# Mixing weights from 16 products over 32 rows, and a tail for the first expert

## The chip, the cores and the metric

The kernel runs on one core of a Trainium2 chip. The time is the device time of one execution in microseconds (us). A run also leaves a profile of one execution, which has a time of its own. Engines are named as in the profile: PE (TensorE, the matmuls), PEld (its weight loads), DVE (VectorE), ACT (ScalarE), POOL (GpSimd), SP (SyncE, which here only issues DMAs).

## What is computed

Two layers of the same form. A mixing step makes a new activation from x, a mixture-of-experts step turns it into an update, and the update is added to x. The change touches only the first layer:

```
att   = softmax(mlp(cond))                        # 32 samples x 8 kernels
agg_w = einsum('bk,koi->boi', att, weight)        # a 64 x 64 mixing matrix for each sample
c0    = einsum('boi,bih->boh', agg_w, x) + att @ bias_k
logits = c0 @ gate_w                              # 2048 tokens, 8 experts
topv, topi = top_k(logits, 2);  w = softmax(topv)
x = x + sum over the two experts e of a token:  w_e * (c0 @ expert_w[e])
```

x is 32 samples x 64 channels x 1024, so 2048 tokens of 1024 features. The second layer mixes with a grouped convolution, has one shared 1024 x 1024 product and LoRA products for each expert.

## The kernel before

Tokens lie in 16 tiles of 128 rows (two samples each).

**Start.** SP loads constants, tile 0, more constants, tile 1, the mixing kernels `kern` (four DMAs of 8 partitions each, line 453), then tiles 2 to 15. PE computes the small network for `att` (lines 1321 to 1325). ACT and DVE make `att_rep`, the attention repeated in four groups of 8 rows, and a product with the identity turns it (L1408) into `att_t`. PE transposes tile 0 and tile 1, four 128 x 128 blocks at a time (`turn_x`, L1339), and ACT copies each batch out of the one bank that they share (`take_turned`, L746), so PE's next batch waits for ACT. Then come 64 mixing products (L1425): for each of 16 output channels o of a group and each of four row groups g, 8 rows of kernels (stationary, 128 columns) times 8 rows of `att_t` (moving, 32 columns). They fill banks 0 to 3. ACT (L767) and DVE (L935) spread these into `bd`, block-diagonal matrices. `gate_products(0)` (L1353) needs all four batches of the first two tiles, and everything of the loop needs `bd`.

**Loop.** For each pair of tiles: transposes, gate products, mixing (`mix`, L1376), logits, top 2, ranks, and the lists of tokens by expert. ACT stores c0 to DRAM. Beside it expert 0's weights are split into a rounded part `w_hi` and the rest `w_lo`.

**Experts.** The tokens of an expert are worked off in slots of 128. POOL gathers the rows of a slot from DRAM (`gather`, L640), one slot ahead, into the one buffer `xg`. PE transposes them in the middle of the slot before (`transposes`, L1472), ACT and DVE split them into `l_hi` and `l_lo`, and PE runs 2 x 24 products of 128 x 512 (`product`, L1481). Meanwhile the weights of the next expert are rounded by ACT (`round_w`, L798) and their rest is made by DVE (`rest_w`, L1098), while SP loads those of the expert after. For experts 2 to 7, the last up to 32 tokens of an expert, its tail, can be left out of the slots: they are gathered together (L668, two gathers, issued by POOL between the slots of expert 0 and those of expert 1, once expert 1's weights are all split, `s_lo`), turned in `turn_tails` (L1508, L1514) behind expert 0's last slot, copied by ACT (L847) and DVE (L1119, L1122), and multiplied in fp32 with the raw weights, in four column groups of 32 (`tail`, L1529), half before and half after the first slot of the expert before. ACT evicts a tail (`take_tail`, L810) and stores it. The number of slots of an expert is computed on the chip: one for each 128 begun, of its count less 32 where it has a tail, at least 3 for experts 0 and 7 and 2 for the others. With the inputs here there are 33 slots, 5 of them expert 0's.

**Order.** Each engine's queue is written out by hand and runs in order; semaphores tie them together. After the experts come the sum of the two experts' rows for each token, and the second layer (conv L1561, down L1570, main L1481, up L1577).

Of the kernel before, what the change touches and what calls it, by code (L numbers as in the profile page):

```python
# [24 lines left out]
TAIL, PLAIN = 32, 2  # L25
GROUPED = E - PLAIN
# [22 lines left out]
QO = CH // QUAD  # L49
# [5 lines left out]
def columns(widths):  # L55

    at, out = 0, {}
    for name, w in widths:
# [7 lines left out]
                    ("thr", NT - 1), ("cw", CH), ("fside", CH), ("tok", NT), ("pick", E)])  # L66
# [32 lines left out]
def build(nc, x, x_t, kern, x_ph, consts_a, consts_b, expert_w, conv_w, down_w, lora_b, out):  # L99
    ctx = ExitStack()  # L100
    with ctx:
# [12 lines left out]
        y_d = dram("y_scratch", [(SLOTS + 1) * P + (E - 2) * TAIL, H])  # L114
# [42 lines left out]
        def row(i, n=1):  # L157
            return work[:, i * H:(i + n) * H]
# [5 lines left out]
        kern_sb = row(4, 2).rearrange("p (o i) -> p o i", o=QO)  # L164
# [29 lines left out]
        att_rep = early[0:B, 10 * P:11 * P]  # L194

# [15 lines left out]
        tail_out = sb("spare", [P, SPARE])[:, 0:H // QUAD]  # L211
        scratch = sb("scratch", [P, E * HG])
        attx = scratch[0:B, :].rearrange("p (n k) -> p n k", k=K8)
        att_t = sb("att_t", [P, B])
# [30 lines left out]
        tail_f = sb("tail_f", [P, GROUPED])  # L245
# [100 lines left out]
        s_txt = [sem(f"s_txt_{j}") for j in range(3)]  # L346
        s_tprod = sem("s_tprod")
        s_tev = sem("s_tev")
# [52 lines left out]

        def places(e):

            return max(e - 1, 0) * TAIL if isinstance(e, int) else e * TAIL - TAIL
# [34 lines left out]
        def _(sp):  # L439
# [53 lines left out]
            sp.wait_ge(s_tplace, 2)  # L493
# [11 lines left out]
            def late_loads():  # L505
# [3 lines left out]
                behind = sp.value_load(cum[0:1, PLAIN:PLAIN + 1], min_val=sum(LEAST[:PLAIN]), max_val=SLOTS)  # L509
                sp.dma_start(y_d[bass.ds(sp.snap(behind * P), TAIL), :], ca[0:TAIL, 0:H]).then_inc(s_rest, 16)  # L510
# [9 lines left out]
            def fill(part):  # L520
# [3 lines left out]
                with sp.Fori(*at) as g:  # L524
                    sp.dma_start(y_d[bass.ds(sp.snap(g * P + (E - 2) * TAIL), P), :], ca[:, 0:H]).then_inc(s_rest, 16)
# [5 lines left out]
            def expert(e, first, last, between=None):  # L531
# [9 lines left out]
                if not last:  # L541
# [5 lines left out]
                    if first:  # L547

                        sp.wait_ge(s_tturn, 3)
                    load_raw(nxt2, range(4, 6))  # L550

            def first_rows():

                sp.wait_ge(s_tprod, 2 * GROUPED)
# [73 lines left out]
        def _(pool):  # L628
            pool.memset(att_rep, 0.0).then_inc(s_init, 1)
# [67 lines left out]
            pool.wait_ge(s_tst, 16 * GROUPED + DMA_CREDIT)  # L697
# [25 lines left out]
        def _(act):  # L723

            act.wait_ge(s_init, 5)
# [36 lines left out]
            for n in range(4):  # L762
                take_turned(0, n)
# [983 lines left out]
```

## Time and profile before

| | us |
|---|---|
| median of 3 runs | 816.88 |
| lowest, highest | 813.99, 818.6 |
| profiled execution, its time | 816.01 |
| profiled execution, its span | 814.3 |

The span runs from the first to the last instruction. Its stages: start to about 26 us, loop to 98, experts to 518, then the second layer. A name such as L1425 is a line of the kernel. In the rows, `out<-in` are the program's names, `x128` is a number of instructions (an fp32 product is recorded as two matmuls and two weight loads), and a bracket gives the idle time of the engine ahead of the row and what ended it. A busy engine that is not on the chain of work that ended last costs nothing.

### The profile page before, as it was taken

The page shows a single profiled execution, that of the slowest core. Times are in us where ns is not written, and L with a number is a line of the kernel's source. Part 1 is how long each engine was busy: PE and PEld are TensorE (multiplying, and loading weights), DVE is VectorE, ACT ScalarE, POOL GpSimd, SP SyncE. Part 2 cuts the span into 40 slices and gives each one's busy share as a digit, 9 for nine tenths or more (in the row PEclk, how much of TensorE's full clock was granted, in tenths as well). Part 3 has the DMA queues.
Part 4 walks back from the last instruction along what each step waited for, and adds up shares of the span by engine and source line. Part 5 has one row for each costly group of instructions (what it writes and reads, how often), then busy time and mean ns, then how long its engine had stood idle before and what let it go on. Part 6 is the DMA issues. An engine that isn't in the chain of part 4 may idle for free.

```text
span 814.3 us, 13091 instructions
## 1 busy us (share of the span) xinstructions
PE 792.2 (97%) x4450; PEld 646.0 (79%) x4450; DVE 394.7 (48%) x921; ACT 208.1 (26%) x326; POOL 86.2 (11%) x130
## 2 busy tenths in 40 slices
PE   7999899999999999999999999999999999999997
PEld 5555588778777787787877878888898889889886
DVE  1488733241331512315123153386676757678883
ACT  3444233341332523325233151300100001001200
POOL 1000112001101111011110112221112111100000
PEclk9999999999999999999999999999999999999999
DMA  9998398468474583745537255765544664432065
GB/s 269 392 342 308 114 320 318 144 196 313 127 273 162 186 324 118 269 174 173 202 111 260 93 182 168 240 178 129 126 103 113 152 148 103 106 98 56 1 219 195
DMA packets 62924, 152.77 MB, mean 188 GB/s; under 512 B 7192, under 2 KB 24616, under 8 KB 61960
## 3 DMA queue, kind: packets, MB, share of 16 engines
q1 hardware_dynamic: 42928, 99.31, 38.1%
q0 software_dynamic: 9616, 34.88, 13.8%
q10 hardware_dynamic: 10344, 18.10, 6.0%
q8 instruction: 22, 0.36, 0.2%
q14 instruction: 14, 0.11, 0.0%
HBM read 99.43 MB, written 44.44 MB: 177 GB/s over the span
## 4 chain that ended last, share of the span: by engine, by line
PE 91%; DMA 4%; DVE 1%; ACT 1%; issue 1%; SPq 1%; POOL 0%; ACTq 0%; POOLq 0%; DVEq 0%
PE bank L1481 63%; PE bank L1561 6%; PE bank L1570 4%; PE bank L1472 4%; PE bank L1376 4%; PE bank L1529 3%; PE bank L1577 3%; DMA work<-c_scratch,idx 2%; PE bank L1353 1%; PE bank L1400 1%; DMA work<-y_scratch,pos_c 1%; PE bank L1425 1%; PE bank L1339 1%; DMA x1p<-res 1%; PE bank L1365 1%
## 5 line engine op out<-in xcount | busy, mean ns | idle before, releaser
L1481 PE MATMUL bank<-weights,l_hi 128*128 128x512 f32 x1568 | 483.3, 389 | 0.0
L1481 PEld LDWEIGHTS bank<-weights,l_hi 128*128 128x128 f32 x1568 | 294.4, 188 | 59.5
L1481 PE MATMUL bank<-weights,l_lo 128*128 128x512 f32 x784 | 311.1, 397 | 1.1 <-DVE l_lo L1065 1.1
L1481 PEld LDWEIGHTS bank<-weights,l_lo 128*128 128x128 f32 x784 | 147.3, 188 | 34.7 <-issue 6.2
L1065 DVE TENSOR_TENSOR l_lo<-bank,l_hi 128x512 fp32r<-128x512 f32 x33 | 22.9, 693 | 185.7 <-ACT l_hi L786 185.7
L1098 DVE TENSOR_TENSOR weights<-work,weights 128x1024 fp32r<-128x1024 f32 x48 | 55.9, 1220 | 23.1 <-ACT weights L798 23.1
L1561 PE MATMUL bank<-conv_sb,x1p 128*128 128x128 f32 x512 | 59.8, 275 | 2.5 <-DMA x1p<-res 1.3
L1561 PEld LDWEIGHTS bank<-conv_sb,x1p 128*128 128x128 f32 x512 | 58.7, 192 | 3.0 <-DMA x1p<-res 1.6
L640 POOL DMA_INDIRECT work<-c_scratch,idx x33 | 34.4, 1043 | 233.4 <-PE bank L1472 139.9
L1223 DVE TENSOR_TENSOR res<-bank,res 128x512 f32 (+1 forms) x30 | 31.9, 1064 | 54.5 <-PE bank L1481 43.5
L1070 DVE TENSOR_TENSOR l_lo<-bank,l_hi 128x512 fp32r<-128x512 f32 x33 | 22.8, 692 | 64.7 <-ACT l_hi L791 64.7
L872 ACT ACTIVATE l_hi<-work 128x512 fp32r<-128x512 f32 x32 | 18.4, 623 | 134.2 <-PE bank L1481 128.0
L798 ACT ACTIVATE weights<-work 128x1024 fp32r<-128x1024 f32 x48 | 47.3, 1047 | 16.1 <-issue 15.7
L786 ACT ACTIVATE l_hi<-bank 128x512 fp32r<-128x512 f32 x34 | 20.4, 599 | 101.9 <-PE bank L1481 92.3
L830 ACT ACTIVATE work<-bank 128x512 f32<-128x512 f32 x33 | 19.6, 595 | 93.9 <-PE bank L1481 83.0
L791 ACT ACTIVATE l_hi<-bank 128x512 fp32r<-128x512 f32 x34 | 20.3, 598 | 70.0 <-PE bank L1481 70.0
L1570 PE MATMUL bank<-down_sb,work 128*128 128x160 f32 x256 | 37.5, 299 | 0.6 <-DVE hb L1189 0.6
L1175 DVE TENSOR_TENSOR work<-bank,ctxb 128x512 f32<-128x512 f32 x32 | 33.5, 1130 | 8.6 <-PE bank L1561 7.8
L1472 PEld LDWEIGHTS bank<-ca,work 128*128 128x128 f32 x272 | 31.7, 140 | 7.5 <-issue 2.3
L1570 PEld LDWEIGHTS bank<-down_sb,work 128*128 128x128 f32 x256 | 36.1, 190 | 1.9 <-issue 0.8
L1472 PE MATMUL bank<-ca,work 128*128 128x128 f32 x272 | 35.4, 272 | 2.1 <-DMA work<-c_scratch,idx 2.1
L690 POOL DMA_INDIRECT work<-y_scratch,pos_c x32 | 33.0, 1031 | 26.2 <-POOL pos_c L685 9.7
(204 smaller groups left out, 603.2 us busy)
## 6 DMA issues: line engine op xcount, KB each, us to landing
work<-in_expert_w SPq DMA_DIRECT2D x52, 512.0 KB, 5.6
y_scratch<-work ACTq DMA_DIRECT2D x66, 256.0 KB, 3.4
x1p<-in_expert_w SPq DMA_DIRECT2D x20, 512.0 KB, 8.0
y_scratch<-ca SPq DMA_DIRECT2D x18, 512.0 KB, 10.1
res<-in_x SPq DMA_DIRECT2D x16, 512.0 KB, 15.1
c_scratch<-work SPq DMA_DIRECT2D x16, 512.0 KB, 3.7
res<-in_x_ph SPq DMA_DIRECT2D x14, 512.0 KB, 5.6
x1p<-res SPq DMA_DIRECT2D x112, 64.0 KB, 4.8
```

The costliest lines, as they stand in the source:

```text
L640: pool.indirect_dma_start(xg, None, c0_d, bass.IndirectOffsetOnAxis(ap=idx[:, 0:1], axis=0)).then_inc(s_xg, 16)
L690: pool.indirect_dma_start(yg[j][:, k, :], None, y_d, bass.IndirectOffsetOnAxis(ap=pos_c[j][:, k:k + 1], axis=0)).then_inc(s_yg[j][k], 16)
L798: act.activation(w_hi[1 - odd][:, at, :], raw[buffer(at)], ACT.Copy).then_inc(s_hi, 1)
L1098: dve.tensor_tensor(w_lo[1 - odd][:, at, :], raw[buffer(at)], w_hi[1 - odd][:, at, :].bitcast(F32), ALU.subtract).then_inc(s_lo, 1)
L1175: dve.tensor_tensor(out4[:, b], ps, add.unsqueeze(2).to_broadcast([P, CQ, HC, CP]), ALU.add).then_inc(s_c1, 1)
L1223: dve.tensor_tensor(to[:, w, :], bank[h][:, :].rearrange("p (w q) -> p w q", q=PH), rows[:, w, :], ALU.add).then_inc((s_me0, s_me1)[h], 1)
L1376: mm = pe.matmul(bank[2 * j + h][:, :], bd[:, t, :], x_sb[t][:, h * HALF:(h + 1) * HALF], start=True, stop=True)
L1472: mm = pe.transpose(bank[bk][:, k * P:(k + 1) * P], xg[:, at * P:(at + 1) * P], ident)
L1481: mm = pe.matmul(to[:, :], a[:, k, :], b[:, k, cols * HALF:(cols + 1) * HALF], start=(k == 0 and n == 0), stop=(k == HC - 1 and n == 2 and ...
L1529: mm = pe.matmul(bank[4][g * TAIL:(g + 1) * TAIL, 0:H // QUAD], tail_xt[:, e - PLAIN, k, :], raw[buffer(k)][:, g * (H // QUAD):(g + 1) * ( ...
L1561: mm = pe.matmul(bank[to + b][:, at:at + P], x1p[j][:, b, u, m * P + k:(m + 1) * P + k], conv_sb[:, k, u, :], start=(k == 0), stop=(k == W ...
L1570: mm = pe.matmul(bank[2][:, 0:G1W], c1_of(t)[:, k, :], down_sb[:, k, :], start=(k == 0), stop=(k == HC - 1))
```

## The change

**Mixing weights.** The 8 kernels of four output channels are laid into the 32 rows of a row group, so 16 products take the place of 64: 32 rows of kernels (stationary, 128 columns) times 32 rows of `att_own` (moving, 128 columns), which is the attention repeated over all rows and multiplied by a mask (`own`) that keeps it in the columns of its own channel. The kernels are loaded by one DMA over 128 partitions, ahead of tile 1. The products stand ahead of tile 1's transposes in PE's queue, and ACT's block copies stand between and behind the copies of tile 1's last batches. POOL's memset of `att_rep` is dropped.

**First expert's tail.** Expert 0 gets a tail too. Its rows are gathered as the seventh tail, in the second gather. It is multiplied behind `turn_tails` with `w_hi[0]` and `w_lo[0]`, read as fp32, both into bank 5 (`first_tail`, 64 products), since the raw weights are gone by then. All four copies of turned tails are waited for. ACT evicts bank 5 and stores it, and expert 2's tail on PE waits for that eviction. Places and counts follow: a tail's rows stand behind each expert but expert 1.

```diff
             load_x(0)
             sp.dma_start(ca[:, mlp:CA_W], consts_a[:, mlp:CA_W]).then_inc(s_const, 16)
+            sp.dma_start(kern_sb, kern.rearrange("p (o i) -> p o i", o=QUAD)).then_inc(s_kern, 16)
             load_x(1)
-            for g in range(QUAD):
-                sp.dma_start(kern_sb[g * QP:g * QP + K8, :, :], kern[g, :, :].rearrange("k (o i) -> k o i", o=QO)).then_inc(s_kern, 16)
...
@@ scalar
-            for n in range(4):
+            for n in range(3):
                 take_turned(0, n)
             act.wait_ge(s_pe0, 7)
-            for g in range(QUAD // 2, QUAD):
-                for b in range(2):
-                    act.activation(*block(g, b), ACT.Copy).then_inc(s_bda, 1)
+            for b in range(2):
+                act.activation(*block(QUAD - 2, b), ACT.Copy).then_inc(s_bda, 1)
+            take_turned(0, 3)
+            for b in range(2):
+                act.activation(*block(QUAD - 1, b), ACT.Copy).then_inc(s_bda, 1)
...
-            act.wait_ge(s_tturn, 1)
-            act.activation(tail_xt[:, 0:QUAD, 0:HC // 2, :], bank[4][:, :].rearrange("p (k i m) -> p i k m", k=HC // 2, i=QUAD),
-                           ACT.Copy).then_inc(s_txt[0], 1)
-            with act.Fori(0, GROUPED // 2) as pair:
+            for n in (0, 2):
+                act.wait_ge(s_tturn, n + 1)
+                act.activation(*turned_tails(n), ACT.Copy).then_inc(s_txt[n], 1)
+            act.wait_ge(s_tprod0, 1)
+            act.activation(first_tail_out, bank[5][:, 0:H // QUAD], ACT.Copy).then_inc(s_tev, 1)
+            act.wait_ge(s_tev, 1)
+            rows = bass.ds(act.snap(act.value_load(cum[0:1, 1:2], min_val=LEAST[0], max_val=SLOTS) * P), TAIL)
+            act.dma_start(y_d[rows, :].rearrange("r (g n) -> g r n", g=QUAD), first_tail_out).then_inc(s_tst0, 16)
+            with act.Fori(0, E // 2 - 1) as pair:
...
@@ vector
-            dve.tensor_copy(att_t[:, :], bank[6][:, 0:B]).then_inc(s_att, 1)
+            dve.tensor_tensor(att_own.rearrange("p (o n) -> p o n", o=QUAD), bank[6][:, 0:B].unsqueeze(1).to_broadcast([P, QUAD, B]),
+                              c("own").unsqueeze(2).to_broadcast([P, QUAD, B]), ALU.mult).then_inc(s_att, 1)
...
-            ch.add(dve.tensor_tensor(cmp[:, 0:PLAIN, :], bank[4][:, 0:PLAIN].unsqueeze(2).to_broadcast([P, PLAIN, NT - 1]),
-                                     c("thr").unsqueeze(1).to_broadcast([P, PLAIN, NT - 1]), ALU.is_gt))
...
+            for some in (slice(0, 1), slice(2, E)):
+                n = some.stop - some.start
+                ins = dve.scalar_tensor_tensor(cmp[:, some, :], bank[4][:, some].unsqueeze(2).to_broadcast([P, n, NT - 1]),
+                                               float(-TAIL), c("thr").unsqueeze(1).to_broadcast([P, n, NT - 1]),
+                                               ALU.add, ALU.is_gt)
...
@@ tensor
+            pe.wait_ge(s_kern, 16)
+            pe.wait_ge(s_att, 2)
+            pe.wait_ge(s_ctx0, 1)
+            for o in range(QUAD):
+                for g in range(QUAD):
+                    rows = slice(g * QP, (g + 1) * QP)
+                    mm = pe.matmul(bank[g][:, o * P:(o + 1) * P], kern_sb[rows, o, :], att_own[rows, :], start=True, stop=True)
+            mm.then_inc(s_pe0, 1)
             turn_x(0, 2)
             turn_x(0, 3)
-            pe.wait_ge(s_kern, 16 * QUAD)
-            pe.wait_ge(s_att, 2)
-            pe.wait_ge(s_ctx0, 1)
-
-            for o in range(QO):
-                for g in range(QUAD):
-                    rows = slice(g * QP, g * QP + K8)
-                    mm = pe.matmul(bank[g][:, o * B:(o + 1) * B],
-                                   kern_sb[rows, o, :],
-                                   att_t[rows, :], start=True, stop=True)
-            mm.then_inc(s_pe0, 1)
             gate_products(0)
...
             def tail(e, half):
-                if e == PLAIN:
-                    for taken in s_txt[0:1] if half == 0 else s_txt[1:]:
-                        pe.wait_ge(taken, 1)
-                elif half == 0:
-
-                    pe.wait_ge(s_tev, e - PLAIN)
+                if half == 0:
+
+                    pe.wait_ge(s_tev, e - 1)
...
+            def first_tail():
+
+                for taken in s_txt:
+                    pe.wait_ge(taken, 1)
+                for k in range(HC):
+                    for n, part in enumerate((w_hi[0], w_lo[0])):
+                        for g in range(QUAD):
+                            mm = pe.matmul(bank[5][g * TAIL:(g + 1) * TAIL, 0:H // QUAD], tail_xt[:, TAILED.index(0), k, :],
+                                           part[:, k, g * (H // QUAD):(g + 1) * (H // QUAD)].bitcast(F32),
+                                           start=(k == 0 and n == 0), stop=(k == HC - 1 and n == 1))
+                mm.then_inc(s_tprod0, 1)
...
             one_expert(pe, experts_slot, 0, 0)
             turn_tails()
+            first_tail()
```

## Rows read from the trace of the kernel before

**Rows 1.** Page, parts 1 and 4: busy time of engines; chain that ended last

```profile
PE 792.2 (97%) x4450; PEld 646.0 (79%) x4450; DVE 394.7 (48%) x921; ACT 208.1 (26%) x326; POOL 86.2 (11%) x130
...
PE 91%; DMA 4%; DVE 1%; ACT 1%; issue 1%; SPq 1%; POOL 0%; ACTq 0%; POOLq 0%; DVEq 0%
```

**Rows 2.** Busy time by stretch: us, engines (instructions), clock, DMA share, GB/s

```profile
9.00:12.00 3.00, 3.00 (x11) 1.84 (x9) 0.48 (x3) 0.60 (x1) 0.00 (x0) 1.00 0.97 128
...
26.00:98.00 72.00, 65.39 (x368) 38.11 (x368) 54.77 (x275) 30.51 (x46) 2.18 (x2) 1.00 0.77 291
```

**Rows 3.** Timeline, start: start us, us, engine, line, operation, [idle before <- releaser]

```profile
12.40 1.12 PE L1339 MATMUL bank<-ca,res 128*128 128x128 f32 x4
...
13.55 0.60 ACT L746 ACTIVATE work<-bank 128x512 f32<-128x512 f32 x1 [3.89 <-PE bank L1339]
...
14.20 1.11 PE L1339 MATMUL bank<-ca,res 128*128 128x128 f32 x4 [0.69 <-ACT work L746]
...
15.25 7.05 PE L1425 MATMUL bank<-att_t,work 8*128 8x32 f32 x128
...
22.23 1.90 PE L1353 MATMUL bank<-work,ca 128*8 128x256 f32 x16
...
22.77 1.19 ACT L767 ACTIVATE bd<-bank 64x256 f32<-64x256 f32 x3
...
25.84 3.27 PE L1376 MATMUL bank<-res,bd 128*128 128x512 f32 x4
...
29.75 1.10 PE L1376 MATMUL bank<-res,bd 128*128 128x512 f32 x2
```

**Rows 4.** Source lines 1425 and 1481: weight loads, duration ns min/median/max

```profile
L1425 PEld LDWEIGHTS bank<-att_t,work x128: 283/328/328, 15.2 to 21.8; 8*128 8x128 f32 x128
...
L1481 PEld LDWEIGHTS bank<-weights,l_hi x1568: 187/188/192, 98.3 to 808.6; 128*128 128x128 f32 x196
```

**Rows 5.** Chain that ended last: start us, us, what; slots and a tail half

```profile
128.35 10.90 PE bank L1481 x48
...
140.13 10.90 PE bank L1481 x48
...
173.83 1.86 PE bank L1529 x32
```

**Rows 6.** Timeline: the tails' copy on ACT and the first tail products

```profile
159.23 0.60 ACT L847 ACTIVATE work<-bank 128x512 f32<-128x512 f32 x1 [0.68 <-PE bank L1514]
...
159.88 1.93 PE L1529 MATMUL bank<-work 128*32 128x256 f32 x32 [1.00 <-ACT work L847]
```

**Rows 7.** Timeline of POOL: the row gathers of expert 0

```profile
117.36 1.05 POOL L640 DMA_INDIRECT work<-c_scratch,idx  x1 [2.01 <-PE bank L1472]
...
125.65 0.34 POOL L654 COPY idx<-idx_all 128x1 int32 x1 [7.24 <-DMA work<-c_scratch,idx]
...
137.73 0.94 POOL L668 DMA_INDIRECT x1p<-c_scratch,tail_idx  x1 [7.54 <-issue]
...
139.88 0.19 POOL L654 COPY idx<-idx_all 128x1 int32 x1
...
141.02 0.97 POOL L640 DMA_INDIRECT work<-c_scratch,idx  x1 [0.95 <-PE bank L1472]
...
147.02 0.18 POOL L654 COPY idx<-idx_all 128x1 int32 x1 [5.03 <-DMA work<-c_scratch,idx]
```

**Rows 8.** Timeline: last rest of expert 1's weights; transposes in slot 3

```profile
127.00 2.35 DVE L1098 TENSOR_TENSOR weights<-work,weights 128x1024 fp32r<-128x1024 f32 x2
...
139.09 1.03 PE L1472 MATMUL bank<-ca,work 128*128 128x128 f32 x8
```

**Rows 9.** Busy time by stretch, columns as in rows 2, over those gathers

```profile
128.00:136.00 8.00, 8.00 (x39) 6.66 (x37) 2.74 (x4) 1.89 (x4) 1.05 (x1) 1.00 0.98 394
```

**Rows 10.** Timeline of ACT: a tail's eviction, its store, the next eviction

```profile
179.37 0.36 ACT L810 ACTIVATE spare<-bank 128x256 f32<-128x256 f32 x1
...
182.15 0.60 ACT L830 ACTIVATE work<-bank 128x512 f32<-128x512 f32 x1 [2.42 <-PE bank L1481]
```

More of the change, by code:

```diff
@@ L24 @@
 FILLS = 4
[L25 to L26 removed]
+TAIL = 32
+TAILED = [2, 3, 4, 5, 6, 7, 0]
+GROUPED = len(TAILED)
 HC = H // P
@@ L345, in build @@
         s_tturn = sem("s_tturn")
-        s_txt = [sem(f"s_txt_{j}") for j in range(3)]
+        s_txt = [sem(f"s_txt_{j}") for j in range(4)]
         s_tprod = sem("s_tprod")
+        s_tprod0 = sem("s_tprod0")
+        s_tst0 = sem("s_tst0")
         s_tev = sem("s_tev")
@@ L508, in late_loads @@
                 sp.wait_ge(s_const, 16)
[L509 to L510 removed]
+                behind = sp.value_load(cum[0:1, 2:3], min_val=sum(LEAST[:2]), max_val=SLOTS)
+                sp.dma_start(y_d[bass.ds(sp.snap(behind * P + TAIL), TAIL), :], ca[0:TAIL, 0:H]).then_inc(s_rest, 16)
                 sp.dma_start(cb[:, :], consts_b).then_inc(s_late, 16)
@@ L810, in take_tail @@
                 act.activation(tail_out, bank[4][:, 0:H // QUAD], ACT.Copy).then_inc(s_tev, 1)
-                wait_apart(act, s_tev, e)
-                behind = act.value_load(cum[0:1, bass.ds(e + 2, 1)], min_val=PLAIN, max_val=SLOTS)
-                rows = bass.ds(act.snap(behind * P + e * TAIL), TAIL)
+                wait_apart(act, s_tev, e + 1)
+                behind = act.value_load(cum[0:1, bass.ds(e + 2, 1)], min_val=sum(LEAST[:3]), max_val=SLOTS)
+                rows = bass.ds(act.snap(behind * P + e * TAIL + TAIL), TAIL)
                 act.dma_start(y_d[rows, :].rearrange("r (g n) -> g r n", g=QUAD), tail_out).then_inc(s_tst, 16)
@@ L1117, in _ @@
                 rest_b(g + 1)
-            dve.wait_ge(s_tturn, 2)
-            dve.tensor_copy(tail_xt[:, 0:QUAD, HC // 2:HC, :],
-                            bank[5][:, :].rearrange("p (k i m) -> p i k m", k=HC // 2, i=QUAD)).then_inc(s_txt[1], 1)
-            dve.wait_ge(s_tturn, 3)
-            dve.tensor_copy(tail_xt[:, QUAD:GROUPED, :, :],
-                            bank[6][:, :].rearrange("p (k i m) -> p i k m", k=HC, i=GROUPED - QUAD)).then_inc(s_txt[2], 1)
-            with dve.Fori(0, GROUPED // 2) as pair:
+            for n in (1, 3):
+                dve.wait_ge(s_tturn, n + 1)
+                dve.tensor_copy(*turned_tails(n)).then_inc(s_txt[n], 1)
+            with dve.Fori(0, E // 2 - 1) as pair:
                 for odd in (1, 0):
@@ L1528, in tail @@
                     for g in range(QUAD):
-                        mm = pe.matmul(bank[4][g * TAIL:(g + 1) * TAIL, 0:H // QUAD], tail_xt[:, e - PLAIN, k, :],
+                        mm = pe.matmul(bank[4][g * TAIL:(g + 1) * TAIL, 0:H // QUAD], tail_xt[:, TAILED.index(e), k, :],
                                        raw[buffer(k)][:, g * (H // QUAD):(g + 1) * (H // QUAD)], start=(k == 0), stop=(k == HC - 1))
                 mm.then_inc(s_tprod, 1)
+            def first_tail():
+                for taken in s_txt:
+                    pe.wait_ge(taken, 1)
+                for k in range(HC):
+                    for n, part in enumerate((w_hi[0], w_lo[0])):
[4 more added lines that the diff above has]
+                mm.then_inc(s_tprod0, 1)
             def experts_slot(g, e, odd, first):
-                tailed = first and PLAIN <= e + 1 < E
+                tailed = first and 2 <= e + 1 < E
                 if tailed:
```

91 lines of the change are left out of this document (47 added, 44 removed).

## Prediction

> **What bounds the kernel now.** I read the page first: the tensor engine (PE) is busy for 97% of the span and is 91% of the chain that ended last [rows 1]. So time goes only where PE has less to do or stops waiting, and each part of the change has to be looked up in its own stretch. The busy times by stretch show that the loop over the tiles (26 to 98 us) holds PE for 65.4 of 72 us, with DMA at 0.77 of its engines and the vector engine (DVE) at 54.8 [rows 2]. PE sets its pace too, so what the start gains is carried through. Then comes the timeline of the start. PE turns tile 1 in two batches (12.40 and 14.20), each followed by a copy on the scalar engine (ACT), runs the 64 mixing products in 7.05 us, and ends with the first gate products at 24.13 [rows 3]. A reader should see that nothing lies between these pieces. Last, the chain in the experts' stage: one slot is 48 products and 8 transposes, and begins every 140.13 - 128.35 = 11.78 us [rows 5].
>
> **Part 1, the mixing products.** Removed: 64 products, which the trace records as 128 (two for each fp32 product), 7.05 us [rows 3]. Added: 16 products, 32 records, each with 128 moving columns where there were 32. A record of 512 columns takes 3.27/4 = 0.82 us in this stretch [rows 3], so one of 128 takes 0.20 and 32 in a row 6.5 us. The four row groups can run abreast. The nearest row is that of the gate products: they run in four column groups, their 16 records of 256 columns would be 16 x 0.41 = 6.5 us in a row and took 1.90, which is 3.4 abreast [rows 3]. By this the new products take 6.5/3.4 = 1.9. The bounds are 1.6 (four abreast) and 6.5 (none); I take 2.0, near the gate products, since those too use a quarter of the array each.
>
> The products also move ahead of tile 1's transposes. They start where those started, at 12.4, and end at 14.4. Both batches with their copies took 15.95 - 12.40 = 3.55 (second batch 14.20 + 1.11, copy 0.60 and a hand-over), so they end at 17.95, and the gate products, 1.90, at 19.85 [rows 3]. Before it was 24.13: a gain of 4.3 us. Of the four copies of mixing blocks on ACT, 0.4 each [rows 3], two now stand ahead of the last copy of tile 1. They need 0.8 and have 1.1, the time of PE's second batch, so they cost nothing; without that cover 0.8. The other two are done under the gate products. The same holds for DVE's four. DVE's copy of the weights becomes a multiplication by a mask over 128 columns. DVE takes 1.2 us over 1024 columns [rows 8], so this is below 0.3, and PE has three products of its own to do meanwhile: nothing.
>
> On SP's queue the mixing kernels now go ahead of tile 1, as one load over 128 partitions in place of four over 8. In the stretch where those landed DMA was taken at 0.97 but moved 128 GB/s [rows 2]. Tile 1 comes behind 256 KB more, but is wanted 2 us later than before; the tiles behind it come sooner. Nothing is waited for there now, so I take 0, with bounds of 0 and a loss of 0.5.
>
> **Part 2, the first expert's tail.** The router of the reference sends 516 tokens to expert 0, which is 4 x 128 + 4. A tail of up to 32 makes 4 slots of 5: 11.78 us less [rows 5]. Added on PE: 64 tail products. A tail half of 16 products takes 1.86 [rows 5], so four times that, 7.44. They wait for all four copies of turned tails where the first half now waits for one of them. ACT does that copy in 0.60 and PE starts 0.05 behind it [rows 6]; ACT now has a second one of 3/4 the size: 0.45. Behind the 64 products PE has a new wait for their eviction, which holds up expert 2's tail and the slot behind it: 0.36 on ACT [rows 10] and two hand-overs, 0.5 together. Sum: 11.78 - 7.44 - 0.45 - 0.5 = 3.4 us gained. On ACT the eviction, its store and the bookkeeping take 182.15 - 179.37 = 2.8 us [rows 10] before the rounding of expert 2's weights; PE meanwhile has a tail half and half a slot, 7.5 us, and the next eviction is wanted only behind these, so it is hidden.
>
> There is a stall to set against it. GpSimd (POOL) fetches rows in one order: gathers 1 to 4 of expert 0, then the two tail gathers, then gather 5. With one slot fewer the tails go ahead of gather 4, which PE wants in the middle of slot 3, at 139.1 [rows 8]. They can't be issued before the rest of expert 1's weights is done (129.35) [rows 8]. The pair and the index copy took 141.02 - 137.73 = 3.3 us [rows 7], so gather 4 goes out at 132.7 (before: 129.14). A gather takes 6.0 us when DMA is quiet (141.02 to 147.02) and 8.3 when it is full (117.36 to 125.65) [rows 7], and over 128 to 136 it is full, 394 GB/s [rows 9]. It lands between 138.7 and 141.0; if the tails' 0.92 MB are in its way, 2.3 us later at that rate, at 143.3. The stall is thus 0 to 4.2 us. I take 1.4, inside the first pair, since the traffic is thinning by then. Part 2 gives 2.0.
>
> Small edits together: one more comparison on DVE ahead of the counts, one more store of zeros, one gather fewer, a tail index more. Each lies beside PE's work; 0, within 0.3.
>
> **A rule against the trace.** Loads and products of one row group: PE's loads of 0.188 us [rows 4] vanish under products that follow each other every 0.227 (24 in 5.45, half of a slot's 10.90 [rows 5]), on the whole array. In the Trainium skill, TensorE: Matmul & The Clock Gate, Part 3 (The mechanism), a weight load overlaps products in flight only if its row group differs. By that rule the eight loads of each group come on top of its products, which is the third rival; the row speaks against it.
>
> **The sum.** 816.0 (the profiled execution; its span is 814.3, with 1.7 around it) - 4.3 - 2.0 = 809.7. The three runs have a median of 816.9, 0.9 above, and lie 4.6 apart; set against their median it is 810.6. I take 810.2.
>
> **The rivals.**
> (1) The row groups don't run abreast: 6.5 in place of 2.0, 814.7. For it: the old records follow each other every 0.055 us, and 32 columns take 0.05, so the old rows would look the same if only the loads ran abreast. Against it: the column groups do run abreast.
> (2) Late gather, the other side: the software queue keeps the pace that it has beside full traffic, 0.52 MB in about 6.7 of the 8.3 us. The tails and gather 4, 1.44 MB, would take 18 us from 130.3 and PE would stall until 149, 10 us: 818.8. It is slower than before once gather 4 lands after 147. Against it: the quiet gather took 6.0 [rows 7].
> (3) Loads of one row group don't hide: 8 x 0.33 [rows 4] + 8 x 0.20 = 4.2 in place of 2.0, 812.4.
> (4) PE's clock. The 512-column records take 0.82 us at 25.84 and 0.55 at 29.75 [rows 3], the slow ones those of the 1.2 GHz level, though the column of granted clock says 1.00 [rows 2]. I assume that the rise comes with the same work as before. If it comes at the same time, 4.3 us more are spent at the slow level and half is lost: 812.3.
> (5) The dense products bring the rise forward: transposes, gate products and first mixes run faster by 3.9: 806.3.
> (6) The slot isn't saved. From 545 tokens for expert 0 there would still be 5 slots, and the tail would cost 8.4 with no gain: 820.5. The count of 516 speaks against it.
>
> **How the numbers follow.** Forecast 0.60; rivals in order 0.07, 0.05, 0.06, 0.12, 0.07, 0.03. A measurement of this kernel tells about 0.5% (4.1 us) from no change, so faster means below 812.8. That is nearly all of the forecast, all of (5), most of (3) and two thirds of (4): 0.77. Within 0.5%: (1), the rests of (3) and (4), half of (2): 0.17. Slower: 0.06. The range: from 806.0 (no stall, three and a half groups abreast, part of (5)) to 815.0 (stall of 4, or (1) or (4)).
>
> **What would show it.** Right: 32 records at line 1425's successor in about 2 us, starting at 12.4; gate products ending near 20; the loop's steps unchanged but 4 us earlier; 32 gathers of slots; 128 tail records in 7.4; in slot 3 a wait for DMA of 1 to 2 us ahead of the transposes. Wrong, if the products take over 4 us, if the loop's end has moved by less than 3.5, if that wait is over 4, or if expert 0 keeps 5 slots.

## The result and the profile after

The changed kernel takes 808.55 us (median of six runs, 806.61 to 810.75), the kernel before beside it 817.0 us (six runs, 813.99 to 820.22). The ratio is 0.990, with a 95% interval of 0.9875 to 0.9917 (6.8 to 10.2 us less). The medians lie 8.5 us apart, where 5.8 to 6.7 were forecast (810.2 against the profiled execution and the median of before). The profiled execution took 806.61 us at a span of 804.9, against 816.01 and 814.3: 9.4 us between the two profiles, a little more than between the medians.

Page of the changed kernel, parts 1, 4 and 5; they answer to [rows 1]:

```profile
span 804.9 us, 13018 instructions
...
PE 780.9 (97%) x4426; PEld 635.9 (79%) x4426; DVE 393.6 (49%) x920; ACT 206.3 (26%) x324; POOL 84.7 (11%) x127
...
PE 90%; DMA 5%; issue 2%; ACT 1%; DVE 1%; SPq 1%; POOLq 0%; POOL 0%; ACTq 0%; DVEq 0%
...
L1498 PE MATMUL bank<-weights,l_hi 128*128 128x512 f32 x1536 | 473.5, 389 | 0.0
...
L648 POOL DMA_INDIRECT work<-c_scratch,idx x32 | 33.4, 1045 | 227.1 <-PE bank L1489 138.8
```

PE bounds this kernel as it did the one before, and its busy time fell by 11.3 us while the span fell by 9.4: the difference is new idle time. The products with l_hi are 1536 in place of 1568, and the gathers of slots 32: expert 0 has four slots.

Timeline of PE at the start of the changed kernel (start us, us, engine, line, operation, count, idle before); it answers to [rows 3]. Line 1442 holds the mixing products, 1356 the transposes, 1370 the gate products, 1393 the mixes:

```profile
11.63 0.59 PE L1442 MATMUL bank<-ctxb,work 32*128 32x128 f32 x3
...
12.01 2.01 PE L1442 MATMUL bank<-ctxb,work 32*128 32x128 f32 x29
13.95 1.11 PE L1356 MATMUL bank<-ca,res 128*128 128x128 f32 x4
15.75 1.12 PE L1356 MATMUL bank<-ca,res 128*128 128x128 f32 x4 [0.69 <-ACT work L755]
17.55 1.90 PE L1370 MATMUL bank<-work,ca 128*8 128x256 f32 x16 [0.69 <-ACT work L755]
...
20.96 1.96 PE L1393 MATMUL bank<-res,bd 128*128 128x512 f32 x4
```

The 32 records run from 11.63 to 14.02. The first three overlap the product ahead of them, and the transposes start at 13.95 where they started at 12.40: 1.55 later, and 1.7 with the 0.16 by which everything from the constants on was early in this execution. The gate products end at 19.45 in place of 24.13, which is 4.7 us. (The block copies of the mixing weights, on ACT and DVE, are not waited for here.) The four mixing records behind them took 1.96 where they took 3.27: here PE's fast level had come before them. The first slot of expert 0 starts at 91.98 in place of 98.19, 6.2 us earlier: the 4.7 are carried through the loop over the tiles, and 1.5 comes in at the mixes.

Timelines of the changed kernel around the first tail, first of POOL, then of PE; they answer to [rows 7] and [rows 8]. Line 676 gathers tails, 648 the rows of a slot, 1489 transposes a slot's rows, 1552 holds the first tail's products and 1541 those of the other tails:

```profile
123.40 0.94 POOL L676 DMA_INDIRECT x1p<-c_scratch,tail_idx  x1 [11.22 <-DVE weights L1118]
124.64 0.91 POOL L676 DMA_INDIRECT x1p<-c_scratch,tail_idx  x1 [0.30 <-issue]
125.56 0.19 POOL L662 COPY idx<-idx_all 128x1 int32 x1
126.71 0.97 POOL L648 DMA_INDIRECT work<-c_scratch,idx  x1 [0.96 <-POOL idx L662]
134.50 0.18 POOL L662 COPY idx<-idx_all 128x1 int32 x1 [6.81 <-DMA work<-c_scratch,idx]
```

```profile
133.99 1.10 PE L1489 MATMUL bank<-ca,work 128*128 128x128 f32 x8 [0.97 <-DMA work<-c_scratch,idx]
...
143.65 7.11 PE L1552 MATMUL bank<-weights,work 128*32 128x256 f32 x128 [1.55 <-ACT work L859]
151.26 1.93 PE L1541 MATMUL bank<-work 128*32 128x256 f32 x32 [0.49 <-ACT spare L861]
153.13 0.50 PE L1498 MATMUL bank<-weights,l_lo 128*128 128x512 f32 x1
```

All the pieces that the sum named are there: the tails go out ahead of gather 4, PE waits 0.97 us for that gather, 128 records take 7.11, and the half tail behind them waits 0.49 for the eviction. From the first slot of expert 0 to the first of expert 1 it is 153.13 - 91.98 = 61.15 us, against 161.75 - 98.19 = 63.56 before: 2.4 us are gained.

The sum of the two profiles is then 6.2 at the start, 2.4 in the first expert, and 0.9 in the last one. There both profiles of before (this one and e8's) have a wait for a gather that no other trace of this case has (timeline of the kernel before):

```profile
485.44 1.09 PE L1472 MATMUL bank<-ca,work 128*128 128x128 f32 x8 [0.66 <-DMA work<-c_scratch,idx]
```

### The profile page after: what moved, and what is told of

Its sections match the earlier page's. It is cut to its first block, busy times and chain, and to the rows that moved or that the text cites. A ratio compares the mean times of both kernels' runs of the same rounds, so it can differ in the third digit from the quotient of the medians.

```text
span 804.9 us, 13018 instructions
## 1 busy us (share of the span) xinstructions
PE 780.9 (97%) x4426; PEld 635.9 (79%) x4426; DVE 393.6 (49%) x920; ACT 206.3 (26%) x324; POOL 84.7 (11%) x127
## 4 chain that ended last, share of the span: by engine, by line
PE 90%; DMA 5%; issue 2%; ACT 1%; DVE 1%; SPq 1%; POOLq 0%; POOL 0%; ACTq 0%; DVEq 0%
PE bank L1498 61%; PE bank L1586 6%; PE bank L1595 4%; PE bank L1393 3%; PE bank L1489 3%; PE bank L1541 3%; PE bank L1602 3%; DMA work<-c_scratch,idx 3%; PE bank L1370 1%; PE bank L1417 1%; PE bank L1552 1%; DMA work<-y_scratch,pos_c 1%; DMA x1p<-res 1%; PE bank L1356 1%; PE bank L1382 1%
## 5 line engine op out<-in xcount | busy, mean ns | idle before, releaser
L1498 PE MATMUL bank<-weights,l_hi 128*128 128x512 f32 x1536 | 473.5, 389 | 0.0
L1498 PEld LDWEIGHTS bank<-weights,l_hi 128*128 128x128 f32 x1536 | 288.4, 188 | 58.3
L1498 PE MATMUL bank<-weights,l_lo 128*128 128x512 f32 x768 | 304.7, 397 | 1.1 <-DVE l_lo L1086 1.1
L1498 PEld LDWEIGHTS bank<-weights,l_lo 128*128 128x128 f32 x768 | 144.2, 188 | 34.0 <-issue 6.2
```

The source lines that it names most:

```text
L1498: mm = pe.matmul(to[:, :], a[:, k, :], b[:, k, cols * HALF:(cols + 1) * HALF], start=(k == 0 and n == 0), stop=(k == HC - 1 and n == 2 and ...
```

## The experiments

Each median stands beside that of the kernel before on the same chip in the same session; ratios are to it, with the 95% interval. PE's granted clock comes into many of them, so it goes first: apart from the edits, executions differ in when PE's clock rises at the start, in whether it drops again, at the first slot above all, and in what follows the last expert.

### The same kernel again: e7, e8, e12

No edit: the changed kernel twice more (the second time also timed), and the kernel before once.

> The changed kernel once more, to see what a second execution does differently. Theory that PE's clock rises at a time that differs between executions of one kernel: the first four mixing records take something other than 1.96 us (the run with part 1 alone, the same up to here, took 3.76), and the first slot begins between 92 and 94. Theory that it rises with the work: 1.96 again and 92.0. The wait of slot 3 should lie between 1.1 and 2.0.

> The kernel before once more. If the rise of the clock is tied to the old products' end it comes near 28.5 us again, as in two of two traces with them in the old place, and the first slot begins at 98.0 to 98.2; if it is free, anywhere from 22 on, and the first slot between 96 and 99. The DMA wait in the last expert (0.8 us before, none in five other traces) should be absent if it was an accident of one execution.

> The changed kernel itself beside the three others and on the same chip, to have its time where theirs is taken: 808.5, within 1.5. Its trace gives one more sample of the clock: rise between 19 and 26 us, and the first slot between 91.7 and 94.2, by which the first slot's step to the next is 7.7 or 9.3.

The changed kernel took 811.39 us in e7 and 807.09 in the profiled execution of e12 (median 808.31, ratio 0.9902 [0.9867, 0.9936] to 816.74). The kernel before took 816.75 in e8. Traces of one program show where such times part. Timeline of e7:

```profile
17.53 1.90 PE L1370 MATMUL bank<-work,ca 128*8 128x256 f32 x16 [0.69 <-ACT work L755]
...
20.99 3.76 PE L1393 MATMUL bank<-res,bd 128*128 128x512 f32 x4
...
92.03 1.07 PE L1489 MATMUL bank<-ca,work 128*128 128x128 f32 x8 [1.55 <-DMA work<-c_scratch,idx]
```

Up to 20.99 it is within 0.03 us of the first trace. Then the same four records take 3.76 us in place of 1.96. By the durations of single records the slow level lasts to about 25.9 in place of 20.9, and the first slot comes at 94.16 in place of 91.98. So 2.2 us at the start are due to the clock's rise alone.

The second difference is at the first slot. Busy times by stretch from 90 to 100 us (length; busy time and instructions of PE, PEld, DVE, ACT, POOL; granted clock; DMA share; GB/s), of the first profile of the changed kernel and of e12:

```profile
90.00:100.00 10.00, 8.94 (x47) 7.43 (x47) 4.67 (x17) 1.90 (x4) 1.98 (x4) 1.00 0.40 124
```

```profile
90.00:100.00 10.00, 8.93 (x41) 7.21 (x40) 4.66 (x17) 1.90 (x4) 1.34 (x3) 0.83 0.39 123
```

Both began the slot at the same point (91.98 and 91.88). In e12 the granted clock of this stretch is 0.83, that is, part of it passed at the 1.2 GHz level. The transposes of the next slot stand 9.30 us behind the first ones, not 7.68: 1.6 us. Ahead of it PE had stood idle for the first gather, but that doesn't separate the two: 1.44 us in the profile without the drop and 1.55 in e6, without it; 1.38 in e12 and 1.55 in e7, with it.

A third difference lies where the change touches nothing. From the last transposes of the experts' stage to the end of the span it is 305.4, 306.1 and 304.3 us in the three traces of the changed kernel, and 305.2 and 303.5 in the two of the kernel before. At least part of it is one wait of PE in the second layer, for a load of x1p from res: 1.6, 1.6 and 0.5 us, and 1.3 and none. Why it varies is open.

What was expected of e8 fell in two points. The clock rose at about 30.6, not near 28.5, and the first slot came at 98.80, outside 98.0 to 98.2: the rise varies in the kernel before too, by 2 us. And the late gather of the last expert was no accident of one profile. It is in this trace too, 2.4 us later, and again costs some 0.7 (steps of 12.40 and 11.85 in place of 11.78). Why only the kernel before shows it is open.

### Part 1 alone, and part 2 alone: e1, e2

e1 is the kernel before with the new mixing products in their new place; all that belongs to tails is as before. e2 is the kernel before with the first expert's tail; all that belongs to mixing is as before.

```diff
 # e1
+            for o in range(QUAD):
                 for g in range(QUAD):
+                    rows = slice(g * QP, (g + 1) * QP)
+                    mm = pe.matmul(bank[g][:, o * P:(o + 1) * P], kern_sb[rows, o, :], att_own[rows, :], start=True, stop=True)
+            turn_x(0, 2)
+            turn_x(0, 3)
...
 # e2
+TAILED = [2, 3, 4, 5, 6, 7, 0]
...
             turn_tails()
+            first_tail()
```

> Part 1 alone: the 16 products, their load, their place and the order of ACT's copies; expert 0 keeps 5 slots without a tail. If the start's gain is carried through as in the traces (98.19 to 91.98 at the first slot): 6.2 us less than before, about 810.8, with a first slot near 92.0 and one DMA wait in the last experts as before. My sum on record had 4.3 for this part; the other 1.9 would be the clock's rise, which came 1.3 to 1.5 us of work earlier in the changed kernel, and 0.3 from the products. If that rise falls at a random time in each execution, the first four mixing records will take 3.27 us here again and the gain is 4.7, about 812.3.

> Part 2 alone: expert 0 has 4 slots and a tail, the 64 old mixing products stay in their place. By the stretches of the two traces (slot 11.8 saved; stall 1.1, copies 0.6, tail products and eviction wait 7.6 added): 2.4 us less in expert 0. If the late row gather in the last expert (PE waited about 0.9 for it before) goes away by this part's shift by one slot, 3.3 less, about 813.7; if it goes by part 1, 2.4 less, about 814.6. The clock rises in the first mixes as before (3.27 us for four records) if the dense old order decides it.

e1: 810.66 us, ratio 0.9929 [0.9903, 0.9955] to 816.2, that is 5.5 us less. e2: 815.13, ratio 0.9995 [0.9977, 1.0013]: a difference from before can't be shown. The sum expected 4.3 and 2.0. By the medians part 1 brings more by itself and part 2 less, but the interval of e1 (3.7 to 7.9 us) holds 4.3, and that of e2 (from 1.9 less to 1.1 more) just misses 2.0. e2 lies above both of its expectations (813.7 and 814.6).

Timeline of e1, then of e2, at the start:

```profile
17.62 1.89 PE L1354 MATMUL bank<-work,ca 128*8 128x256 f32 x16 [0.69 <-ACT work L744]
...
21.08 3.76 PE L1377 MATMUL bank<-res,bd 128*128 128x512 f32 x4
```

```profile
15.20 7.05 PE L1442 MATMUL bank<-att_t,work 8*128 8x32 f32 x128
22.18 1.90 PE L1370 MATMUL bank<-work,ca 128*8 128x256 f32 x16
...
25.79 3.10 PE L1393 MATMUL bank<-res,bd 128*128 128x512 f32 x4
```

e1's gate products end at 19.51 and its first slot is at 93.94: 4.6 and 4.3 us ahead of before. In this execution the rise didn't come ahead of the mixes, and these took 3.76 where before's took 3.27, so the 4.3 of the first slot are the forecast's number partly by chance. e1's time came out as its first theory had it (810.8), its trace as the second (3.76, and not a first slot near 92.0); the late gather is gone from it, as from e2. Part 2 in the traces is read from the first slot to the last transposes of the experts' stage: 410.0 in e1 and 407.6 in the changed kernel, so 2.5 us; e2 shows 408.4, so 1.6. The stall there was larger (timeline of e2):

```profile
140.53 1.09 PE L1489 MATMUL bank<-ca,work 128*128 128x128 f32 x8 [1.51 <-DMA work<-c_scratch,idx]
```

The slot's step is 13.44 in place of 11.78, so 1.7 us of stall against 1.1, which is 0.5 of the 0.8 between 1.6 and 2.5. In the medians part 2 on top of part 1 is 810.66 less 808.3 to 808.6, so 2 us, from different sessions and with intervals that overlap; without part 1 it is 1.1, not told from none.

### The old products in the new place, the new ones in the old: e4, e3

e4 is the changed kernel with the 64 products over 8 rows (and their loads), run ahead of tile 1's transposes. e3 is the changed kernel with its 16 products behind these transposes, and ACT's copies in the old order.

```diff
 # e4
-            for o in range(QUAD):
+            for o in range(QO):
                 for g in range(QUAD):
-                    rows = slice(g * QP, (g + 1) * QP)
-                    mm = pe.matmul(bank[g][:, o * P:(o + 1) * P], kern_sb[rows, o, :], att_own[rows, :], start=True, stop=True)
+                    rows = slice(g * QP, g * QP + K8)
+                    mm = pe.matmul(bank[g][:, o * B:(o + 1) * B], kern_sb[rows, o, :], att_t[rows, :], start=True, stop=True)
...
 # e3
+            turn_x(0, 2)
+            turn_x(0, 3)
             for o in range(QUAD):
...
-            turn_x(0, 2)
-            turn_x(0, 3)
```

> The changed kernel with the 64 old products (8 rows, 32 columns) in the new place, kernels loaded ahead of tile 1 in four loads as before. The products take 7.05 in place of 1.7: the first slot comes 5.3 us later than in the changed kernel. Theory that the dense products bring the clock's rise forward: the first four mixing records take 3.27 again, 1.4 more, together 815.3. Rival, that the rise comes at a time of its own: it has come by 20.9, before the first mixes at about 26, so these take 1.96, 813.9. Also the kernels' slow load may be waited for here (up to 2 us).

> The changed kernel with the 16 products and ACT's copies in the old order, behind tile 1's transposes. The move costs PE two waits of 0.69 for ACT's copies that lay beside the 64 products before. Theory: the place gives nothing with short products; gate products end at about 18.9 in place of 19.45, since ACT's last copy of tile 1 is under the products, but the block copies then end only at about 18.6: 0.5 us faster, about 808.0. Rival: the early place is what keeps the block copies off the path, and the old place is 1 us slower, 809.5.

e4: 816.25 us, ratio 0.9999 [0.9975, 1.0023]. With the old products the changed kernel is no faster than the one before: the gain of part 1 is in the products. It is nearly 8 us between the medians of e4 and the changed kernel, more than the 5.0 by which the gate products end later (24.48, not 19.45). Timeline of e4, and its busy times from 29 to 40 us:

```profile
11.95 7.11 PE L1442 MATMUL bank<-att_t,work 8*128 8x32 f32 x125
...
26.05 3.76 PE L1395 MATMUL bank<-res,bd 128*128 128x512 f32 x4
```

```profile
29.00:40.00 11.00, 9.78 (x49) 5.23 (x48) 5.28 (x31) 5.05 (x8) 0.00 (x0) 0.87 0.82 313
```

The mixes ran at the slow level, which lasted to about 30.3, and then the granted clock fell again (0.87). The first slot came at 100.51, 8.5 behind the changed kernel: 5.0 are the products. The other 3.5 are put down to the clock, by its two losses; no run separates them.

e3: 807.88 us, ratio 0.9904 [0.9875, 0.9933], the same as the changed kernel within what can be told. Moving the products ahead of the transposes is not what brings the time. The traces show that it costs a little. Timeline of e3, then the row of e6 (the old order too, with an early rise) that stands behind its gate products:

```profile
14.01 1.11 PE L1354 MATMUL bank<-ca,res 128*128 128x128 f32 x4 [0.69 <-ACT work L755]
15.05 2.09 PE L1442 MATMUL bank<-ctxb,work 32*128 32x128 f32 x32
17.07 1.90 PE L1368 MATMUL bank<-work,ca 128*8 128x256 f32 x16
19.09 0.63 PE L1354 MATMUL bank<-ca,res 128*128 128x128 f32 x4
...
29.25 3.66 PE L1391 MATMUL bank<-res,bd 128*128 128x512 f32 x4
```

```profile
17.03 1.38 PE L1372 MATMUL bank<-work,ca 128*8 128x256 f32 x16
19.05 0.63 PE L1358 MATMUL bank<-ca,res 128*128 128x128 f32 x4 [0.65 <-ACT bd L780]
```

In the old order the mixing products run while ACT copies the second batch of transposes. In the new one PE stands idle for 0.69 us a second time, ahead of the gate products (17.55), where the old order had the mixing products to do. The gate products end at 18.97 in place of 19.45: 0.5 us. But the old order pays some of it back: the block copies can start only behind the products, and PE's next transposes wait for them. They start at 19.09 in e3, at 19.05 in e6 though its gate products ended at 18.41, and at 19.38 in the changed kernel. So on the chain the move loses 0.3, not 0.5. e3's first slot is none the less at 92.85, behind the changed kernel's: in this trace the clock fell again at 29.25, where four records took 3.66 us in place of 1.96. All 32 records take 2.09 us here.

### Gather 4 ahead of the tails, and both edits together: e5, e6

e5 is the changed kernel, with POOL fetching all four slots of expert 0 before the two tail gathers. e6 adds e3's edit to it.

```diff
             with pool.Fori(0, 1) as e:
                 fetch_slots(e, 1)
+            with pool.Fori(1, 2) as e:
+                fetch_slots(e, 0, 1)
             pool.wait_ge(s_lo, 2 * HC)
...
-            with pool.Fori(1, E) as e:
+            with pool.Fori(1, 2) as e:
+                fetch_slots(e, 1)
+            with pool.Fori(2, E) as e:
                 fetch_slots(e, 0)
```

> The changed kernel, but POOL issues gather 4 (the first slot of expert 1) ahead of the two tail gathers. PE waited 1.1 us for gather 4 in slot 3 of the changed kernel, 1.7 to 2.0 in three other runs with the tail. Theory: the tails in front of it are the cause, gather 4 goes out 4 us earlier (beside slot 2's end) and the step from slot 2's transposes to slot 3's falls from 12.9 to 11.8: 1.1 to 2 us faster, about 807.0. Rival: the tail gathers then land too late, since each gather is waited for before the next: they would go out at about 131 and land by 137, PE turns them at 139; if they take 8 us more, the wait only moves there and the time stays at 808.5.

> The old place of the short products (0.7 us faster in the medians, 807.9) and gather 4 ahead of the tails. If the two are independent, the gains add to 2 to 2.5 us against the changed kernel, about 806.3, with neither a wait in slot 3 nor one for a second copy of tile 1. If the old place only seemed faster by the clock's luck, it equals the run with gather 4 first alone.

e5: 807.18 us, ratio 0.9874 [0.9854, 0.9893] to 817.8. e6: 805.42, ratio 0.9854 [0.9832, 0.9876], the fastest median of kernels that do all the work, but for e11's, which is the same within 0.1. Timeline of POOL in e5, then of PE (lines 1489, 1552 and 1541 are 1493, 1556 and 1545 here):

```profile
124.38 0.98 POOL L648 DMA_INDIRECT work<-c_scratch,idx  x1 [0.94 <-PE bank L1493]
133.25 0.94 POOL L678 DMA_INDIRECT x1p<-c_scratch,tail_idx  x1 [7.88 <-issue]
134.49 0.92 POOL L678 DMA_INDIRECT x1p<-c_scratch,tail_idx  x1 [0.30 <-issue]
```

```profile
134.27 1.03 PE L1493 MATMUL bank<-ca,work 128*128 128x128 f32 x8
...
143.86 7.11 PE L1556 MATMUL bank<-weights,work 128*32 128x256 f32 x128 [1.55 <-ACT work L863]
151.47 1.93 PE L1545 MATMUL bank<-work 128*32 128x256 f32 x32 [0.49 <-ACT spare L865]
```

The transposes in slot 3 wait for nothing, and the step is 11.78. The tails, although fetched 10 us later, are there in time: the wait of 1.55 ahead of the tail products is the one for the copies of turned tails, as in the changed kernel. So the stall was real, it cost 1.1 us, and it came from the order on POOL's queue. In the medians it doesn't show by itself: the intervals of e5 and of the changed kernel overlap.

### The prices of the pieces: e9, e10, e11

e9 leaves out 60 of the 64 products of the first tail. e10 counts expert 0 without a tail, so it has five slots and the tail's work besides. e11 is e6, with expert 2's tail no longer waiting for the eviction of the first.

```diff
 # e9
-                for k in range(HC):
-                    for n, part in enumerate((w_hi[0], w_lo[0])):
+                for k in range(1):
+                    for n, part in enumerate((w_hi[0],)):
...
 # e10
-            for some in (slice(0, 1), slice(2, E)):
+            for some in (slice(2, E),):
...
 # e11
-                if half == 0:
+                if half == 0 and e > 2:
                     pe.wait_ge(s_tev, e - 1)
```

> The changed kernel with 4 of the 64 products of the first expert's tail (60 are left out, so the sums of expert 0's last 4 tokens are not the reference's). This prices the products: 7.1 us in the trace. Theory that they lie wholly on PE's path: from the end of expert 0's last slot to the first slot of expert 1 falls from 12.7 us to about 6.0, and the time by 6.6, to about 802.0. Rival that ACT's or SP's next work would hold PE anyway (ACT rounded expert 2's weights only up to 158.7, just when PE wanted its next eviction): part of it comes back and the time stays above 803.5.

> The changed kernel, but expert 0's slots are counted without the 32 rows of its tail, so it keeps 5 slots and the tail products run on rows that nobody reads. This is my sixth rival made on purpose. The slot is worth 11.8 us and with 5 slots the tails are behind gather 4 again, which gives back the wait of 1.1 to 2.0: 10 us more than the changed kernel, 818.5, slower than the kernel before by 0.2%. If the slot were worth less (its gathers and stores beside a full DMA), it would be below 816.

> Old place of the short products, gather 4 first, and expert 2's tail no longer waits for the eviction of the first expert's (they use different banks). The wait that the change added was 0.5 us between the tail products and expert 2's half tail (150.76 to 151.26). Without it the chain is 0.5 shorter: about 805.0 against 805.4 of the kernel without this edit, which a measurement can't tell apart; the trace can: the step from slot 3's transposes to slot 4's falls from 24.64 to 24.1. Rival: ACT, which begins expert 2's rounding no earlier, then holds the next eviction, and the half microsecond comes back at the next use of bank 0.

e9: 803.64 us, ratio 0.9845 [0.9801, 0.9888] to 816.74, 4.7 less than the changed kernel in that session. Timeline of e9:

```profile
143.64 0.64 PE L1552 MATMUL bank<-weights,work 128*32 128x256 f32 x8 [1.55 <-ACT work L859]
145.23 3.26 PE L1541 MATMUL bank<-work 128*32 128x256 f32 x32 [0.95 <-ACT spare L861]
154.00 1.03 PE L1489 MATMUL bank<-ca,work 128*128 128x128 f32 x8
```

The records left out are 7.11 - 0.64 = 6.5 us, yet the next transposes come only 4.7 us sooner (154.00, not 158.71). Of the rest 0.5 is a longer wait for the eviction, which nothing covers now, and 1.3 is the half tail, which took 3.26 in place of 1.93: PE's clock had dropped here, behind two waits of 1.55 and 0.95. So the products are on the path at their full price, and taking them away gives some of it back by the clock. The time is where the rival had it (above 803.5), but these two terms make up the whole difference, not a hold by ACT's rounding.

The start of this trace shows the earliest rise of all, and a second drop:

```profile
14.02 1.04 PE L1356 MATMUL bank<-ca,res 128*128 128x128 f32 x4
15.74 0.66 PE L1356 MATMUL bank<-ca,res 128*128 128x128 f32 x4 [0.69 <-ACT work L755]
17.09 1.05 PE L1370 MATMUL bank<-work,ca 128*8 128x256 f32 x16 [0.69 <-ACT work L755]
...
28.42 3.66 PE L1393 MATMUL bank<-res,bd 128*128 128x512 f32 x4
```

The rise came at about 15, ahead of the gate products, which end 1.3 us sooner than in the changed kernel's first trace. The drop at 28.42 took 1.7 back, and the first slot is at 91.97, where it is with a rise at 20.9.

e10: 817.87 us, ratio 1.0024 [1.0000, 1.0047]. This is rival 6, whose price was 820.5: against the changed kernel it is 9.6 us slower. Its slots follow each other in 11.78 each with no stall, the fifth among them. (Its profiled execution, 823.41, is the slowest of its ten.)

e11: 805.32 us, ratio 0.9849 [0.9816, 0.9881]. Timelines of e6 and of e11 (half tail behind the first tail):

```profile
141.54 7.11 PE L1554 MATMUL bank<-weights,work 128*32 128x256 f32 x128 [1.55 <-ACT work L861]
149.15 1.93 PE L1543 MATMUL bank<-work 128*32 128x256 f32 x32 [0.49 <-ACT spare L863]
```

```profile
143.43 7.11 PE L1554 MATMUL bank<-weights,work 128*32 128x256 f32 x128 [1.55 <-ACT work L861]
150.65 1.93 PE L1543 MATMUL bank<-work 128*32 128x256 f32 x32
```

The wait is gone, and the step falls from 24.64 to 24.25: it was worth 0.4 us, too little for the medians (805.42 and 805.32) to tell. The time doesn't come back behind it, as the rival had it: the step after that is 13.87 in e6 and 13.86 in e11.

## Why the prediction was right, and where its terms were off

**The sum held.** 810.2 was forecast and 808.55 measured, inside 806.0 to 815.0. Both parts work by the mechanism named, and the start and the first expert carry nearly all of the difference.

**The mixing products** were taken at 2.0 us between bounds of 1.6 and 6.5. They cost 1.7 on the path in their new place. From the first record to the last end it is 2.09 in e3, and 2.39 in the changed kernel and e1, where the first three overlap the product ahead. By their columns 32 in a row would take 6.5: the four row groups run abreast. Rival 1 (6.5) falls. So does rival 3, by which the eight pairs of load and product of a group would take 4.2 us: the whole took 2.09 and 2.39. In the Trainium skill, TensorE: Matmul & The Clock Gate, Part 3 (The mechanism), a weight load overlaps products in flight only if its row group differs; the trace doesn't agree with that use of the rule.

**The move** was put into the sum as part of 4.3, and the times at which things follow each other there were rightly worked out. What the working didn't ask is whether the move gains at all. By e3 and e6 it loses 0.3: a wait of 0.69 that the old order had covered, less what the old order spends on the block copies.

**The gate products' end** was expected at 19.85, a gain of 4.3; it came at 19.45, 4.7, with 0.3 from the shorter products and 0.2 from the constants' earlier landing. The block copies on ACT and DVE and the kernels' load cost nothing, as forecast: no wait in this stretch names them.

**PE's clock is the term that was left out.** The forecast assumed that the rise comes with the same work as before, which puts it at nothing; rival 4 set it at the same time as before (812.3), rival 5 ahead of the gate products (806.3). None of the three is how it goes throughout. With the 64 narrow products the slow level lasted to between 28.2 and 30.6 us in all four traces (before, e2, e4, e8). With the 16 wide ones it ended between about 15 (e9) and 26 (e10) in ten traces, at 20.9, 20.8 and 25.9 in three of one kernel. Where it was late (e1, e7, e10), with or just behind the first mixes as before, the first slot stands at 93.9 to 94.2; where it was early it stands at 91.8 to 92.0 in the new order. So in part of the executions 2.2 us more are gained, over half of the 3.9 that rival 5 wanted; once, in e9, the rise came ahead of the gate products as it had said, and a later drop took the rest.

How much of the time this is can be put in numbers. e7 and e8, whose clocks rose within the same group of products, have their first slots 4.64 us apart (94.16 and 98.80): 4.3 of the forecast and 0.3 from the shorter products. On average over the seven traces with the new start, the first slot is at 92.8, over before, e2 and e8 at 98.3: 5.5 us, as in e1's median. By this estimate the clock adds some 0.9 to the start, about half of the 1.7 by which the forecast was high. It is an estimate, from few traces: by the medians alone part 1 (5.5, between 3.7 and 7.9) can't be told from 4.3. Why the rise comes later behind the narrow products isn't settled: the runs show that it goes with them, in either place (e4).

**The first expert.** The step of 11.78 saved and the tail of 7.11 + 0.5 (forecast 7.44 + 0.5) are confirmed by e10 and e9. The second copy cost 0.58 for 0.45. The stall was taken at 1.4 between 0 and 4.2: it was 1.1, 1.2 and 0.75 in the three traces of the changed kernel and 1.7 to 2.0 in e2, e3 and e4. Gather 4 took 7.8 us (126.71 to 134.50), inside the 6.0 to 8.3 read ahead; rival 2, with PE stalled for 10 us, falls, and e5 shows the stall's cause. Part 2 was to give 2.0: it gave 2.4 in the two profiles and about 2 in the medians on top of part 1, where the intervals overlap.

**What the two profiles didn't see, and the sum neither.** Profiled executions of one kernel lie up to 4.8 us apart (806.61 and 811.39), by 2.2 for the rise, 1.6 for the drop at the first slot, 0.8 behind the last expert, and some tenths for the stall. The 9.4 us between the first two profiles hold an early rise, which e7 lacks; the medians show 8.5. The late gather in the last expert (0.9 and 0.7 in the two traces of before, none in the twelve others) stands in no term of the forecast. It seems to be a cost of the kernel before that either part takes away, and so a second piece of what the forecast missed; no run isolates it, and its cause stays open.

## What to carry over

Products that use 32 rows of the array can be spread over its four row groups and run nearly abreast (2.09 us, where one after another they would take 6.5), so 16 wide ones replaced 64 narrow ones at 0.3 of their 7.05 us. When a step becomes shorter, look at what was hidden behind it: the new order lost a cover worth 0.3 us, and a queue that serves two consumers in a fixed order (POOL's gathers) was good for one more microsecond once it was set by who waits first. Compare several traces of one kernel before a difference of 1 to 4 us between two traces is explained, and give a median its interval before it is split into parts.

## What the chip showed that was not expected

The rise of PE's clock at the start varies between executions of one program: the same four records at 20.96 and 20.99 us took 1.96 us in one and 3.76 in another, after 9 us in which the two traces are alike to 0.03 us. In this early stretch the column of granted clock says 1.00 in both, so only the durations show the level.

With the narrow products (8 rows by 32 columns) PE ran on without a gap from 15.25 to 24.13 in the kernel before [rows 3], and the records behind were at the slow level's pace until 28.4. In four traces with them the rise never came before 28.2, in ten with the wide ones always by 26.

The clock can drop at the first slot after an idle time of about 1.4 us ahead of its transposes, and doesn't have to: 1.38 and 1.55 us with a drop (e12 and e7, granted clock 0.83 from 90 to 100 us), 1.44 and 1.55 without (the first trace and e6). It did in six of fourteen traces. A drop costs 1.6 us at the first slot, and in e9 another took 1.3 of the 6.5 that the removed products should have given.
